# VectorE's transposition behind the hidden low parts, and another pacing wait ahead of the loop's down projection, in a one-core block kernel

## The chip, the cores and the metric

The kernel runs on one core of a Trainium2 chip. Its engines each take their own list of instructions in order and meet only at semaphores: TensorE (PE; its weight loads are listed as PEld), VectorE (DVE), ScalarE (ACT), GpSimd (POOL), and SyncE (SP), which issues most of the DMAs. The metric is the device time of one execution in microseconds (us). The kernel before took 506.76 us, the median of three runs from 506.46 to 507.39.

## The reference: what is computed

The input x has 8 sequences of 1024 tokens of 256 features, all float32. Two residual blocks follow each other:

```
x = x + mixer(layernorm(x))
x = x + experts(layernorm(x))

mixer:   xp, z = split(x @ w_in)                  # 256 -> 2 x 512
         xc = silu(depthwise causal convolution of xp, 4 taps, + conv_b)
         h[t] = 0.9 * h[t-1] + 0.1 * (xc[t] @ w_B) # 16 states, a scan over the tokens
         y = (h @ w_C) * silu(z)
         return y @ w_out                          # 512 -> 256
experts: per sequence, the two best of 8 experts by (first token @ Wr + br)
         mean over both of  gelu(x @ W1 + b1) @ W2 + b2
```

## The kernel before, in words

**Precision.** A float32 product is made of three products of a rounded type: each operand is split into a high part (rounded, on ACT) and a low part (the rest, by a subtraction), and PE adds hi x hi, hi x lo and lo x hi. So nearly every tensor that PE reads has a `_hi`, made by ACT, and a `_lo`, made by DVE or POOL. The state's input and output (`state_in`, `state_out`) pack high and low parts into one operand, `b_mix`, `c_mix` and `state_mix`.

**Chunks and steps.** The 8192 tokens are 16 chunks (NC) of 512 tokens, two per sequence. The work is a software pipeline over steps s: in step s, chunk a = s is in the mixer, chunk o = s - 1 has its output projection, residual and second layernorm, and chunk f = s - 2 is in the experts. An opening handles the first chunks; steps 4 to 13 are a hardware loop of five rounds (each an even step, q = 0, then an odd one, q = 1); step 3 and steps 14 to 17 are written out. In the profile step s = 3 reaches down at 100.7 us, step 4 at 131.4, step 8 at 252.9, step 9 at 283.1 and step 14 at 434.9.

**PE's order in a step** (`step` at the end of `tensor`): `xp` (input projection, x half), `out_proj` of chunk o in two halves, `z` (the gate half), `up` of chunk f, `state_in` (four products of `b_mix` with `xc_hi`, L1486, and four with `xc_lo`, L1489), `down` of chunk f: its first half (24 products of 256 columns), 12 products of its second half, then `state_out` (four products, L1510), then down's last 12 products. `down(f, 0, ...)`'s products are L1422 to L1424, in groups of three; 36 of them stand ahead of `state_out` and 12 behind. `down` waits for `g_lo` (the low parts of the hidden layer, `hid_lo`), `state_out` for `h_lo` (the low part of `state_mix`).

**The pacing waits.** PE's instructions are issued ahead of their execution. In front of the first product of `out_proj` and of `down`, PE waits for one of its own earlier products (`behind` with a constant in the written-out steps, `behind_next` with a register in the loop) and then issues a few increments of a semaphore, `paced`, that nobody waits for. `state_tail` is incremented by the first of the four L1489 products, the fourth-last of `state_in`. A wait directly ahead of an increment becomes one instruction with it. So in the loop two semaphore instructions and one register instruction stand between that product's end and down's first weight load, in the written-out steps three semaphore instructions.

**DVE's order in a step** (`step` in `vector`), from the residual on: `residual`, `turn2_lo`, `stats2`, then `stats1` and `moments1` of chunk a + 2, `turn_squares(a + 1)` (L971: transposes the 32 x 32 squares of the normalized chunk that a DMA has regrouped; ACT's `turn1_hi` reads it), `hidden_lo(f)` (four subtractions, L861, each behind ACT's `hid_hi` of that part), `scan(a)` (L1041, the recurrence), `edge` (a small copy), `state_lo(a)` (L861 again, the low part of `state_mix`), `turn1_lo(a + 1)`, `ys(a)` and `finish(f)`. L861 is the line of a helper: the tiles' names tell its uses apart.

**ACT's order** behind the gates: a table load, then for each of four parts the gelu (L728) and its rounding `hid_hi` (L611), `norm2(o)` (L666, four), `state_hi(a)` (L611, `state_mix`, behind the scan), `turn1_hi(a + 1)`. **POOL** in even steps adds `b_sel` to the residual (L498, four) behind all four `hid_lo`; in odd steps it does so earlier, between its other work.

**The chain inside a step** is thus: gelu and `hid_hi` on ACT, `hid_lo` and scan on DVE, `state_hi` on ACT, `state_lo` on DVE, `state_out` on PE.

Of the kernel before, what the change touches and what calls it, by code (L numbers as in the profile page):

```python
# [22 lines left out]
def build_block(nc, x, w_in, conv_w, conv_b, w_B, w_C, w_out, Wr, br, W1, b1, W2, b2, out):  # L23
# [19 lines left out]
    with ExitStack() as ctx:  # L43
# [129 lines left out]


        passed = sem("passed")
        x_tail, state_tail, up_tail = sem("x_tail"), sem("state_tail"), sem("up_tail")
        paced = sem("paced")

# [680 lines left out]
        def _(dve):  # L859
# [286 lines left out]
            def step(s, q, half):  # L1146
                a, o, f = s, s - 1, s - 2
                halves = half - 1 if q == 0 else half
                if q == 0 and not has_attn(s):
                    last_split((1, 2, 3))  # L1150
                    route(half - 1)
                    finish(f - 1, 1, 1)
                    turn2_lo(f)
                    residual(o, 1, halves, 0)
                    residual(o, 1, halves, 1)
                    stats2(o, 1)
                    hidden_lo(f, range(JF))
                    norm2_last()
                    turn2_lo(o)
                    finish(f, 0, 0)  # L1160
                    finish(f, 0, 1)
                    return
                if q == 0:
                    route(half - 1)
                    if has_attn(s):
                        taps(a, 0)
                    turn_squares2(f)
                    if has_attn(s):
                        taps(a, 1)
                    residual(o, 1, halves, 0)  # L1170
                    residual(o, 1, halves, 1)
                    turn2_lo(f)
                    stats2(o, 1)
                    if has_next(s, 2):
                        stats1(a + 2)
                        moments1(a + 2)
                    if has_next(s, 1):
                        turn_squares(a + 1)
                    hidden_lo(f, range(JF))
                    if has_attn(s):  # L1180
                        scan(a, 0)
                    if has_next(s, 1):
                        edge(a + 1, False)
                    if has_attn(s):
                        state_lo(a, 0)
                    if has_next(s, 1):
                        turn1_lo(a + 1)
                    if has_attn(s):
                        ys(a)
                    finish(f, 0, 0)  # L1190
                    finish(f, 0, 1)
                    return
                if not has_attn(s):
                    hidden_lo(f, range(JF))
                    finish(f, 1, 0)
                    finish_tile(f, 1, 2, tok[1])
                    finish_tile(f, 1, 3, turn[0])
                    return
                taps(a, 0)
                if isinstance(a, int) and a == 3:  # L1200
                    taps(a, 1)
                    turn_squares2(f)
                    turn2_lo(f)
                else:
                    turn_squares2(f)
                    taps(a, 1)
                residual(o, 0, halves, 0)
                residual(o, 0, halves, 1)
                if not (isinstance(a, int) and a == 3):
                    turn2_lo(f)  # L1210
                stats2(o, 0)
                if has_next(s, 2):
                    stats1(a + 2)
                if has_next(s, 2):
                    moments1(a + 2)
                if has_next(s, 1):
                    turn_squares(a + 1)
                hidden_lo(f, range(JF))
                scan(a, 1)
                if has_next(s, 1):  # L1220
                    edge(a + 1, True)
                state_lo(a, 1)
                if has_next(s, 1):
                    turn1_lo(a + 1)
                if has_next(s, 1):
                    ys(a)
                    finish(f, 1, 0)
                    finish(f, 1, 1)
                else:
                    finish(f, 1, 0)  # L1230
                    ys(a)
# [5 lines left out]
        def _(pe):  # L1237
            mm = nc.tensor.matmul
            x_nth, state_nth = nc.tensor.alloc_register("x_nth"), nc.tensor.alloc_register("state_nth")
            nc.tensor.reg_mov(x_nth, FIRST + 1)  # L1240
            nc.tensor.reg_mov(state_nth, FIRST + 1)

            def turns(normed, sem_out):
                for k in range(KD):
# [188 lines left out]
            def behind_next(tail, nth):  # L1433
# [3 lines left out]
                    pe.sem_inc(paced, 1)  # L1437
                nc.tensor.reg_add(nth, nth, 1)

            def down_tile(f, n, dst, js=range(JF)):  # L1440
                rows = slice(n * P, (n + 1) * P)
                for j in js:
                    t, cols = j // KD, slice(j % KD * D, (j % KD + 1) * D)
                    mm(dst, hid_hi[:, j, rows], w2_hi[:, t, cols], start=(j == 0), stop=False)
                    mm(dst, hid_hi[:, j, rows], w2_lo[:, t, cols], start=False, stop=False)
                    ins = mm(dst, hid_lo[:, j, rows], w2_hi[:, t, cols], start=False, stop=(j == JF - 1))
                if js[-1] == JF - 1:
                    ins.then_inc(down_ready, 1)

            def down(f, h, js=range(JF), tail=None):  # L1450
                for j in js:
                    if h == 0:
                        pe.wait_ge(g_lo, f * JF + j + 1)
                        if isinstance(f, int) and f == LAST - 1 and j % KD == 0:
                            pe.wait_ge(w2_lo_set, LAST // 2 * TOP_K + j // KD + 1)
                    if j == 0 and tail is not None:
                        if isinstance(f, int):
                            behind(*tail)
                        else:
                            behind_next(state_tail, state_nth)  # L1460
                    t, cols = j // KD, slice(j % KD * D, (j % KD + 1) * D)
                    ins = tokens(h, j, j == JF - 1, hid_hi, hid_lo, w2_hi[:, t, cols], w2_lo[:, t, cols])
                if js[-1] == JF - 1:
                    ins.then_inc(down_ready, 1)
# [17 lines left out]
            def state_in(a):  # L1482
                bank = u_bank(a)
                for j in range(JD):
                    pe.wait_ge(xc_hi_set, a * JD + j + 1)
                    mm(bank[:], b_mix[:, j, :], xc_hi[:, j, :], start=(j == 0), stop=False)  # L1486
                for j in range(JD):
                    pe.wait_ge(xc_lo_set, a * JD + JD if isinstance(a, int) and a < 3 else a * JD + j + 1)
                    ins = mm(bank[:], b_mix[:, j, :], xc_lo[:, j, :], start=False, stop=(j == JD - 1))  # L1489
                    if j == JD - 4:  # L1490
                        ins.then_inc(state_tail, 1)
                ins.then_inc(u_ready, 1)
# [167 lines left out]
```

## Time and profile before

| | |
|---|---|
| median of three runs | 506.76 us (506.46 to 507.39) |
| the profiled execution | 505.8 us, its span 504.0 us |
| granted clock of PE | 0.999 |
| busy: PE, DVE, ACT, POOL | 99%, 90%, 79%, 69% |
| the products' L1510 (`state_out`) | 395 ns mean |
| L1422 in `down` and in `out_proj` | 281 and 278 ns mean |

The span runs from the first to the last instruction of the profiled execution; its own time is 1.8 us longer. Busy time of an engine counts its execution only, with overlapping products counted once. A product's listed duration contains its filling and draining, so products start more closely than they last: the start-to-start distances in the timelines are what PE's time is made of. The same holds for DVE, where an instruction starts a little before the end of the one ahead of it.

### The profile page before, as it was taken

What the parts mean: (1) busy time and instruction counts of PE and PEld (TensorE: products, weight loads), DVE (VectorE), ACT (ScalarE), POOL (GpSimd) and SP (SyncE); (2) the same over time, 40 slices, a digit from 0 to 9 for tenths busy, and PEclk for the clock granted to TensorE, in tenths of its full rate; (3) what the DMA queues carried; (4) which work ended last, traced back from release to release, by engine and by line L of the source; (5) the groups of instructions that cost most, each with busy time, mean ns of one, the idle gap of its engine ahead of it and who ended that gap; (6) DMA issues with size and microseconds to landing.
All of it is one profiled execution on the core that took longest, in us unless ns stands there. A gap on an engine that the chain in (4) does not pass through costs nothing.

```text
span 504.0 us, 9945 instructions
## 1 busy us (share of the span) xinstructions
PE 498.7 (99%) x3026; PEld 440.4 (87%) x3026; DVE 452.9 (90%) x896; ACT 400.2 (79%) x692; POOL 348.7 (69%) x390
## 2 busy tenths in 40 slices
PE   8999999999999999999999999999999999999997
PEld 7888799788888988888888888988889888888997
DVE  6999999989998899989999899998999989996773
ACT  4986959878869788697887969779797888969554
POOL 4959597559693696928969197782977649764291
PEclk9999999999999999999999999999999999999999
DMA  8940105344151532605235160432604333130102
GB/s 259 298 179 6 37 1 179 114 142 153 64 190 42 167 125 83 208 10 199 82 125 166 42 221 28 165 126 83 208 31 136 125 126 126 47 120 1 42 2 85
DMA packets 53380, 57.29 MB, mean 114 GB/s; under 512 B 8682, under 2 KB 49642, under 8 KB 53226
## 3 DMA queue, kind: packets, MB, share of 16 engines
q1 hardware_dynamic: 51498, 56.67, 33.7%
q10 hardware_dynamic: 1856, 0.31, 0.3%
q8 instruction: 13, 0.21, 0.2%
q14 instruction: 13, 0.11, 0.1%
HBM read 35.46 MB, written 21.50 MB: 113 GB/s over the span
## 4 chain that ended last, share of the span: by engine, by line
PE 98%; DVE 1%; DMA 1%; issue 0%; DVEq 0%
PE blk L1299 16%; PE blk L1302 16%; PE blk L1308 16%; PE tok L1422 12%; PE tok L1424 12%; PE tok L1423 11%; PE blk L1510 3%; PE turn L1489 3%; PE turn L1486 3%; PE turn L1246 1%; PE tok L1308 1%; PE tok L1302 1%; PE tok L1299 1%; DMA x_mid<-in_L_attn_x 1%; DVE stats_t L917 0%; DVE normed L934 0%
## 5 line engine op out<-in xcount | busy, mean ns | idle before, releaser
L992 DVE SCALAR_TENSOR_TENSOR conv<-blk,tap_w,conv 128x512 f32<-128x512 f32 x192 | 130.1, 742 | 7.2 <-ACT conv L683 6.3
L488 POOL TENSOR_TENSOR y_lo<-gate,y_hi 128x512 fp32r<-128x512 f32 x57 | 72.2, 1297 | 35.9 <-ACT y_hi L611 35.8
L1299 PE MATMUL blk<-xn_hi,w_in_hi 128*128 128x512 f32 x228 | 89.6, 393 | 0.0
L1302 PE MATMUL blk<-xn_hi,w_in_lo 128*128 128x512 f32 x228 | 89.0, 390 | 0.0
L453 POOL TENSOR_TENSOR xc_lo<-conv,xc_hi 128x512 fp32r<-128x512 f32 x60 | 73.2, 1236 | 7.5 <-ACT xc_hi L611 7.4
L1422 PE MATMUL tok<-w_out_hi,y_hi 128*128 128x256 f32 x256 | 71.1, 278 | 0.0
L1423 PE MATMUL tok<-w_out_lo,y_hi 128*128 128x256 f32 x256 | 70.8, 276 | 0.0
L1424 PE MATMUL tok<-w_out_hi,y_lo 128*128 128x256 f32 x256 | 70.7, 276 | 0.0
L1308 PE MATMUL blk<-xn_lo,w_in_hi 128*128 128x512 f32 x228 | 70.4, 390 | 0.0
L1422 PE MATMUL tok<-w_hi,hid_hi 128*128 128x256 f32 x248 | 69.8, 281 | 0.2
L1424 PE MATMUL tok<-w_hi,hid_lo 128*128 128x256 f32 x248 | 69.3, 279 | 0.0
L1423 PE MATMUL tok<-w_lo,hid_hi 128*128 128x256 f32 x248 | 69.3, 279 | 0.0
L683 ACT ACTIVATE conv<-blk,tap_b,tap_w 128x512 f32<-128x512 f32 x64 | 49.1, 777 | 24.8 <-PE blk L1308 21.4
L689 ACT ACTIVATE conv<-conv 128x512 f32<-128x512 f32 x64 | 39.3, 630 | 30.5 <-DVE conv L992 29.5
L861 DVE TENSOR_TENSOR hid_lo<-hid,hid_hi 128x512 fp32r<-128x512 f32 x64 | 44.8, 732 | 15.5 <-ACT hid_hi L611 15.2
L498 POOL TENSOR_TENSOR x_mid<-x_mid,b_sel 128x256 f32<-128x256 f32 x60 | 45.7, 794 | 13.2 <-DVE hid_lo L861 11.2
L1308 PEld LDWEIGHTS blk<-xn_lo,w_in_hi 128*128 128x128 f32 x228 | 42.8, 188 | 9.1
L1422 PEld LDWEIGHTS tok<-w_out_hi,y_hi 128*128 128x128 f32 x256 | 48.0, 188 | 2.6 <-issue 1.3
L1302 PEld LDWEIGHTS blk<-xn_hi,w_in_lo 128*128 128x128 f32 x228 | 42.8, 188 | 8.0
L1299 PEld LDWEIGHTS blk<-xn_hi,w_in_hi 128*128 128x128 f32 x228 | 42.8, 188 | 8.1
L1422 PEld LDWEIGHTS tok<-w_hi,hid_hi 128*128 128x128 f32 x248 | 46.6, 188 | 3.7 <-issue 2.2
L1299 PE MATMUL blk<-xn_hi,w_hi 128*128 128x512 f32 x124 | 48.4, 390 | 0.0
(189 smaller groups left out, 1320.5 us busy)
## 6 DMA issues: line engine op xcount, KB each, us to landing
spill<-normed SPq DMA_DIRECT2D x25, 512.0 KB, 2.9
normed<-spill SPq DMA_DIRECT2D x100, 128.0 KB, 2.8
out<-x_mid SPq DMA_DIRECT2D x30, 256.0 KB, 2.4
x_mid<-in_L_attn_x SPq DMA_DIRECT2D x29, 256.0 KB, 2.8
x_in<-in_L_attn_x SPq DMA_DIRECT2D x14, 512.0 KB, 3.8
w_all<-in_L_ffn_W SPq DMA_DIRECT2D x2, 2048.0 KB, 11.3
b_all<-in_L_ffn_b SPq DMA_DIRECT2D x1, 1024.0 KB, 13.9
gate<-in_L_attn_w_in SPq DMA_DIRECT2D x2, 256.0 KB, 4.8
```

The lines of the kernel that those rows point to most:

```text
L453: nc.gpsimd.tensor_tensor(xc_lo[:, j, :], conv[:, j, 0:CH], xc_hi[:, j, :].bitcast(F32), ALU.subtract).then_inc(xc_lo_set, 1)
L488: nc.gpsimd.tensor_tensor(y_lo[:, j, :], gate_of(o, j), y_hi[:, j, :].bitcast(F32), ALU.subtract).then_inc(y_lo_set, 1)
L498: ins = nc.gpsimd.tensor_tensor(mid(f, q)[:, n, :], mid(f, q)[:, n, :], b2_sel[:], ALU.add)
L683: nc.scalar.activation(conv[:, j, HALO:HALO + CH], blk[j][:], ACT.Identity, bias=tap_b[:, j:j + 1], scale=tap_w[:, j, 0:1]).then_inc(tap_f ...
L861: return nc.vector.tensor_tensor(dst, src, hi.bitcast(F32), ALU.subtract)
L992: nc.vector.scalar_tensor_tensor(cols, blk[j][:], tap_w[:, j, t:t + 1], cols, ALU.mult, ALU.add).then_inc(tap_added, 1)
L1299: ins = mm(dst, whi(k), his(k), start=(k == 0), stop=False)
L1302: mm(dst, wlo(k), his(k), start=False, stop=False)
L1308: ins = mm(dst, whi(k), los(k), start=False, stop=(k == KD - 1))
L1422: mm(dst, his[:, j, rows], whi, start=(j == 0 and n == 0), stop=False, skip_group_check=True)
L1423: mm(dst, his[:, j, rows], wlo, start=False, stop=False, skip_group_check=True)
L1424: ins = mm(dst, los[:, j, rows], whi, start=False, stop=(last and n == 1), skip_group_check=True)
```

## The change

Two edits. On DVE, in both kinds of step, `hidden_lo(f, range(JF))` is issued ahead of `turn_squares(a + 1)` instead of behind it (the diff shows the even one). On PE, in the loop alone, `down` waits for another product: the fourth of the four L1486 products increments the new semaphore `state_fifth` by 2; `behind_fifth` counts a register up by one, waits for `state_fifth`, issues three increments, counts the register up again, and waits once more (for the same increment by 2) with one more increment. The written-out steps keep `behind` and `state_tail`.

```
-                    if has_next(s, 1):
-                        turn_squares(a + 1)
                     hidden_lo(f, range(JF))
+                    if has_next(s, 1):
+                        turn_squares(a + 1)
                     if has_attn(s):
                         scan(a, 0)
...
-            nc.tensor.reg_mov(state_nth, FIRST + 1)
+            nc.tensor.reg_mov(state_nth, 0)
...
+            def behind_fifth(tail, nth):
+                pe.sem_inc(paced, 1)
+                nc.tensor.reg_add(nth, nth, 1)
+                pe.wait_ge(tail, nth)
+                for _ in range(PACE):
+                    pe.sem_inc(paced, 1)
+                nc.tensor.reg_add(nth, nth, 1)
+                pe.wait_ge(tail, nth)
+                pe.sem_inc(paced, 1)
...
-                            behind_next(state_tail, state_nth)
+                            behind_fifth(state_fifth, state_nth)
...
-                    mm(bank[:], b_mix[:, j, :], xc_hi[:, j, :], start=(j == 0), stop=False)
+                    ins = mm(bank[:], b_mix[:, j, :], xc_hi[:, j, :], start=(j == 0), stop=False)
+                if not isinstance(a, int):
+                    ins.then_inc(state_fifth, 2)
```

## Rows read from the trace of the kernel before

**Rows 1.** Page, parts 1 and 4: busy time of TensorE; chain of work by engine.

```profile
PE 498.7 (99%) x3026; PEld 440.4 (87%) x3026; DVE 452.9 (90%) x896; ACT 400.2 (79%) x692; POOL 348.7 (69%) x390
...
PE 98%; DVE 1%; DMA 1%; issue 0%; DVEq 0%
```

**Rows 2.** Timeline of VectorE, step 9: start, us taken, operation, count, [idle before].

```profile
278.95 1.24 DVE L971 STREAM_TRANSPOSE normed<-normed 128x1024 f32<-128x1024 f32 x1
280.11 1.27 DVE L861 TENSOR_TENSOR hid_lo<-hid,hid_hi 128x512 fp32r<-128x512 f32 x2
...
283.17 0.69 DVE L861 TENSOR_TENSOR hid_lo<-hid,hid_hi 128x512 fp32r<-128x512 f32 x1 [0.55 <-ACT hid_hi L611]
283.78 1.27 DVE L1041 TENSOR_TENSOR_SCAN state<-decay,state,turn 128x512 f32<-128x512 f32 x1
...
285.75 0.69 DVE L861 TENSOR_TENSOR state_mix<-state,state_mix 64x512 fp32r<-64x512 f32 x1 [0.63 <-ACT state_mix L611]
```

**Rows 3.** Timeline of ScalarE, step 9: the fourth hid_hi, and state_mix.

```profile
282.51 0.63 ACT L611 ACTIVATE hid_hi<-hid 128x512 fp32r<-128x512 f32 x1
...
285.09 0.63 ACT L611 ACTIVATE state_mix<-state 128x512 fp32r<-128x512 f32 x1
```

**Rows 4.** Timeline of TensorE, step 9: down, state_out, down's last 12.

```profile
283.13 0.28 PE L1422 MATMUL tok<-w_hi,hid_hi 128*128 128x256 f32 x1
...
287.37 1.09 PE L1510 MATMUL blk<-state_mix,c_mix 128*128 128x512 f32 x4
288.29 0.28 PE L1422 MATMUL tok<-w_hi,hid_hi 128*128 128x256 f32 x1
```

**Rows 5.** Timeline of VectorE, step 8.

```profile
251.52 2.47 DVE L861 TENSOR_TENSOR hid_lo<-hid,hid_hi 128x512 fp32r<-128x512 f32 x4
253.92 1.21 DVE L1041 TENSOR_TENSOR_SCAN state<-decay,turn 128x512 f32<-128x512 f32 x1
...
255.83 1.03 DVE L861 TENSOR_TENSOR state_mix<-state,state_mix 64x512 fp32r<-64x512 f32 x1 [0.18 <-ACT state_mix L611]
```

**Rows 6.** Timeline of ScalarE, step 8: the fourth hid_hi.

```profile
252.29 0.63 ACT L611 ACTIVATE hid_hi<-hid 128x512 fp32r<-128x512 f32 x1
```

**Rows 7.** Timeline of TensorE, step 8: state_out and down's last 12.

```profile
257.15 1.09 PE L1510 MATMUL blk<-state_mix,c_mix 128*128 128x512 f32 x4
258.08 0.28 PE L1422 MATMUL tok<-w_hi,hid_hi 128*128 128x256 f32 x1
```

**Rows 8.** Timelines of VectorE and TensorE, step 6.

```profile
195.18 1.02 DVE L861 TENSOR_TENSOR state_mix<-state,state_mix 64x512 fp32r<-64x512 f32 x1 [0.20 <-ACT state_mix L611]
...
197.27 0.28 PE L1422 MATMUL tok<-w_hi,hid_hi 128*128 128x256 f32 x1
```

**Rows 9.** Line L971 alone: count, shortest/median/longest in ns, first and last start.

```profile
L971 DVE STREAM_TRANSPOSE normed<-normed x12: 1231/1235/1240, 98.3 to 429.6; 128x1024 f32<-128x1024 f32 x12
```

**Rows 10.** Timelines of TensorE and ScalarE, step 14.

```profile
434.94 0.28 PE L1422 MATMUL tok<-w_hi,hid_hi 128*128 128x256 f32 x1
...
439.06 1.09 PE L1510 MATMUL blk<-state_mix,c_mix 128*128 128x512 f32 x4
...
434.32 0.63 ACT L611 ACTIVATE hid_hi<-hid 128x512 fp32r<-128x512 f32 x1
```

**Rows 11.** Timelines of ScalarE and TensorE, step 4.

```profile
130.49 0.63 ACT L611 ACTIVATE hid_hi<-hid 128x512 fp32r<-128x512 f32 x1
...
131.40 0.35 PE L1422 MATMUL tok<-w_hi,hid_hi 128*128 128x256 f32 x1
...
136.65 0.28 PE L1422 MATMUL tok<-w_hi,hid_hi 128*128 128x256 f32 x1
```

**Rows 12.** Timeline of GpSimd, step 8: its four adds.

```profile
254.16 3.29 POOL L498 TENSOR_TENSOR x_mid<-x_mid,b_sel 128x256 f32<-128x256 f32 x4 [2.05 <-DVE hid_lo L861]
```

**Rows 13.** Timeline of VectorE, start of step 8: a tap waits for ScalarE.

```profile
233.00 0.75 DVE L992 SCALAR_TENSOR_TENSOR conv<-blk,tap_w,conv 128x512 f32<-128x512 f32 x1 [0.61 <-ACT conv L683]
```

**Rows 14.** Line L1437 alone, a semaphore instruction of the pacing: ns, starts.

```profile
L1437 PEldq EVENT_SEMAPHORE  x40: 51/51/51, 112.4 to 404.1; - x40
```

More of the change, by code:

```diff
@@ L175, in build_block @@
         passed = sem("passed")
+        state_fifth = sem("state_fifth")
         x_tail, state_tail, up_tail = sem("x_tail"), sem("state_tail"), sem("up_tail")
@@ L1176, in step @@
                         moments1(a + 2)
+                    hidden_lo(f, range(JF))
                     if has_next(s, 1):
                         turn_squares(a + 1)
-                    hidden_lo(f, range(JF))
                     if has_attn(s):
@@ L1215, in step @@
                     moments1(a + 2)
+                hidden_lo(f, range(JF))
                 if has_next(s, 1):
                     turn_squares(a + 1)
-                hidden_lo(f, range(JF))
                 scan(a, 1)
```

## The prediction

> **What bounds the kernel now.** Read the chain of work that ended last first: TensorE (PE) holds 98% of it [rows 1], so what counts is only what leaves PE idle or slows its products. VectorE (DVE) is no bound of its own, but every hand-over inside a step goes through it. Steps are named by s = a, as in the code (s = 4 to 13 are the loop). All sums below are made inside one step, from the timelines, on the stretch from the end of ScalarE's (ACT) fourth hid_hi to the start of down's last 12 products (first L1422 after L1510).
>
> Odd step s = 9, in order of time. DVE does the transposition L971, then hid_lo (four L861), idles 0.55 us before the last of them until ACT's fourth hid_hi is there, then scan L1041, then the low part of state_mix [rows 2]. ACT ends the fourth hid_hi at 283.14 and rounds state_mix from 285.09 [rows 3]. PE starts down at 283.13, state_out at 287.37 and down's last 12 at 288.29 [rows 4]. The low part of state_mix is ready at 285.75 + 0.69 = 286.44, 0.93 us before state_out takes it. That 0.93 is the cover that matters. In the even step s = 8 it is 257.15 - 256.86 = 0.29 (state_out starts 0.93 before 258.08) [rows 5, 7].
>
> How close may it get? In s = 6 the low part ends at 195.18 + 1.02 = 196.20 and down's last 12 start at 197.27 [rows 8]: 1.07 after it. In s = 9 that distance is 288.29 - 286.44 = 1.85. State_out's four products alone take 0.92 (288.29 - 287.37), so in s = 6 PE went on 0.15 after the data, and I take 1.07 as the price from the data to PE going on.
>
> **Part 1, hidden_lo ahead of turn_squares.** Nothing is added; DVE's order changes from L971, L861 x4, L1041 to L861 x4, L971, L1041, in every step from 3 to 14 (12 transpositions, 1.235 us each [rows 9]). In the odd step the transposition now runs in time in which DVE would otherwise wait for ACT: it ends before hid_lo, and the fourth hid_lo starts 0.03 after ACT's fourth hid_hi. That instant is ACT's and does not move. Behind it the new order puts the whole transposition, 280.11 - 278.95 = 1.16 us start to start, in front of the scan.
>
> The new sum for an odd step, from the end of the fourth hid_hi: 0.03 to hid_lo's start (283.14 to 283.17), 0.61 to the next DVE instruction (283.17 to 283.78), 1.16 for the transposition, 1.27 for the scan, 0.04 to ACT (285.05 to 285.09), 0.63 for its rounding, 0.03 back to DVE, 0.69 for the low part, 1.07 for state_out [rows 2, 3, 8]. Together 5.53 us. Before it was 288.29 - 283.14 = 5.15. So 0.38 us is lost on PE in each odd step: the 1.16 less the unused cover.
>
> Even step: the scan takes 1.21 instead of 1.27 [rows 5], so the new stretch is 5.47. Before: s = 8 258.08 - 252.92 = 5.16 [rows 6, 7], loss 0.31; s = 6, 10 and 12 were not worked out one by one; s = 14, by its rows, 439.06 + 0.92 - 434.95 = 5.03, loss 0.44 [rows 10]. I take the middle, 0.37, for each of the five (6, 8, 10, 12, 14). s = 4 is another case: down starts only at 131.40, late against ACT's fourth hid_hi at 131.12, since hid_lo is late there; the old stretch is 136.65 - 131.12 = 5.53 [rows 11]. The new order takes that lateness away and puts the other in its place: -0.06. s = 3 has no row here; with a late hid_lo too, its bounds are -0.06 (as s = 4) and 0.38 (as an odd step); I take 0.2.
>
> One thing decides what an even step costs. Its low part of state_mix takes 1.03 us instead of the odd step's 0.69, with GpSimd's (POOL) four adds L498 running from 254.16 to 257.45 beside it [rows 5, 12]; in the odd step POOL does them elsewhere. The adds start 0.17 after the last hid_lo (253.99). In the new order the last hid_lo ends at 252.95 + 0.69 = 253.64, so the adds run from 253.81, 0.35 earlier, and end at 257.1 at the latest, while the low part starts later, at 256.63 instead of 255.83. I take 0.69; with the old duration it is 0.34 more per even step. Bounds: 0.69 and 1.03. The Trainium skill, SBUF — State Buffer, "Who interferes with whom", says of this case that a VectorE instruction with two SBUF inputs and a GpSimd one that reads SBUF exclude each other, and the one issued second waits for the whole of the first. The trace agrees with a wait of that kind (0.34 us more); by this rule the low part would run free once the adds are through, and be held about as long as the fourth add still has to run, which puts the even step between my two bounds.
>
> Who else waits for DVE? The transposed normed1 is read by ACT's turn1_hi, which stands behind state_hi in ACT's order, and state_hi itself waits for the scan: no further wait. After state_out DVE's xn_lo, ys and finish come later by about what PE comes later, and in front of its next taps DVE waits 0.61 us for ACT [rows 13], which takes up the rest. SP and POOL lose no time in front of PE: no DMA is issued at another place in its queue. Cost: 0; without that cover, see the rivals.
>
> **Part 2, the pacing wait of down in the loop.** Ten times, PE waits for the fourth high product, which is one product (0.23 us, 0.92 for four) earlier than before, and then has four semaphore instructions (the waiting one counted) and one register instruction where it had two and one, and one register instruction more ahead of the wait. Each semaphore instruction is 51 ns in its row [rows 14]; what it holds the queue for is not seen. Bounds for the start of down: earlier than now by 0.23 - 0.10 = 0.13, with which down runs as now; or later by 0.2. The aim can be read from PE's rows: the 36 products before state_out take 287.37 - 283.13 = 4.24 in the loop, but 439.06 - 434.94 = 4.12 in s = 14, which has three semaphore instructions and no register instruction [rows 4, 10]. So a gain up to 0.12 per step, 1.1 in nine steps. But it lies ahead of state_out, and state_out now waits for the low part: in the odd step ready at 283.14 + 5.53 - 1.07 = 287.60, where down ends at 287.37 + 0.2 at the latest. Gain and loss both disappear in the wait. I take 0.
>
> **Sum.** Odd 5 x 0.38 = 1.9, even 5 x 0.37 = 1.85, s = 3 +0.2, s = 4 -0.06: 3.9 us. The profiled execution took 505.8 us with a span of 504.0; the span would become 507.9. The median of the runs shown is 506.76, 0.96 above the profiled one; the difference is added to it: 510.7.
>
> **The rivals.**
> 1. *Contention stays.* The low part of state_mix takes 1.03 in all six even steps: 6 x 0.34 = 2.0 more, 512.7. For it: all even steps shown have it. Against: the adds move forward, the low part back.
> 2. *The transposition is hidden after all (the other side).* The place is state_out's wait for the low part of state_mix. It decides at the point where that is ready 0.1 to 0.3 us ahead of state_out's planned start. If the delay stayed below the cover (0.93), PE would keep its beat, the late starts of s = 3 and 4 would go (5.53 - 5.15 = 0.38, and 0.2), and the pacing could bring its 1.1: 505.1, faster; without the pacing 506.2, the same. For it: DVE idles 0.55 before its last hid_lo. Against: that idle time is before the fourth hid_lo, and 1.16 is more than 0.93.
> 3. *The delay accumulates.* DVE carries it into its taps and PE waits in the next step as well; nothing of it is covered. At the full 1.16 for six odd steps (3 with them) and 253.92 to 254.72, 0.80, for six even ones: 11.8 us, 518.6. Against: the 0.61 us in front of the taps, and PE itself is later.
> 4. *The change does not pace.* The new wait passes too early: as said, no time.
>
> **How the numbers follow.** Forecast with rival 4: 0.73. Rival 1: 0.12. Rival 3: 0.05. Rival 2: 0.10, of which 0.06 with the pacing (faster) and 0.04 without (same). Less than 0.2% (1.0 us) cannot be told from no change here. Faster 0.06, same 0.04, slower 0.90. Low end: 1.07 could be 0.1 less with PE's queue empty, 11 x 0.1 = 1.1 less, and s = 3 at nothing: 509.4. High end: rival 1 and a little: 512.9.
>
> **What would show it.** DVE's timeline: L971 between the fourth hid_lo and L1041, the scan of odd steps 1.80 instead of 0.64 us after the fourth hid_hi. PE's waits: a new entry, L1510 (or its weight load) for DVE's state_mix, some 0.4 us each in about 11 steps; the share of PE busy falls below 99%. POOL's adds in even steps end before or at the start of the low part, which is 0.69. If L1510 shows no wait, or if PE's lost time sits at L1299 or L1422 of the next step, the forecast is wrong.

## The result, and the profile after

The changed kernel took 513.63 us, the median of four runs (512.02 to 514.2), against 506.77 (506.46 to 507.39, four runs) of the kernel before: a ratio of 1.0129, 95% interval 1.0104 to 1.0153. It is slower by 6 to 7 us; forecast were 3.9, with 512.9 us as the high end. The profiled execution took 512.02 us, its span is 510.2 instead of 504.0: 6.2 more, and this is what the sums below account for. The other three executions took 513.59 to 514.2; they were not traced, and the 0.6 us between 6.2 and the 6.9 of the medians stays open. The granted clock was 0.999 before and 1.000 after, so it is not the clock. Lines behind the edits are numbered higher after: L971 is L972, L861 is L862, L1041 is L1042, L1422 to L1424 are L1423 to L1425, L1510 is L1524.

The page after: the span, busy times, and the chain of work by engine. Those of before are [rows 1].

```profile
span 510.2 us, 9985 instructions
...
PE 501.6 (98%) x3026; PEld 439.7 (86%) x3026; DVE 451.7 (89%) x896; ACT 399.9 (78%) x692; POOL 346.7 (68%) x390
...
PE 59%; DVE 20%; issue 10%; ACT 9%; DMA 1%; DVEq 0%
```

TensorE held 98% of the chain; now it holds 59%, because in every step the chain leaves TensorE for VectorE's `hid_lo`, transposition and scan, ScalarE's rounding and VectorE's low part. In step 9 it comes to them from ScalarE's gelu; in step 8 it is on ScalarE and VectorE almost throughout from 234.3 us, where the taps wait for the input projection. The waits say where it comes back. Of TensorE and its weight loads the first two rows for `state_out` are these (us in all, times, the longest); before there was none for this line.

```profile
PE blk L1524 <- DVE state_mix L862: 3.0, 10, 0.4
...
PEld blk L1524 <- DVE state_mix L862: 5.5, 12, 0.6
```

**An odd step**, s = 9, VectorE's timeline (start, us taken, operation, count, [idle before]). It answers to [rows 2].

```profile
284.88 0.69 DVE L862 TENSOR_TENSOR hid_lo<-hid,hid_hi 128x512 fp32r<-128x512 f32 x1 [0.55 <-ACT hid_hi L612]
286.12 0.69 DVE L862 TENSOR_TENSOR hid_lo<-hid,hid_hi 128x512 fp32r<-128x512 f32 x1 [0.55 <-ACT hid_hi L612]
286.73 1.24 DVE L972 STREAM_TRANSPOSE normed<-normed 128x1024 f32<-128x1024 f32 x1
287.90 1.24 DVE L1042 TENSOR_TENSOR_SCAN state<-decay,state,turn 128x512 f32<-128x512 f32 x1
...
289.83 0.69 DVE L862 TENSOR_TENSOR state_mix<-state,state_mix 64x512 fp32r<-64x512 f32 x1 [0.63 <-ACT state_mix L612]
```

And TensorE's, which answers to [rows 4]:

```profile
290.58 1.21 PE L1524 MATMUL blk<-state_mix,c_mix 128*128 128x512 f32 x4 [0.22 <-DVE state_mix L862]
291.63 0.28 PE L1423 MATMUL tok<-w_hi,hid_hi 128*128 128x256 f32 x1
```

The fourth `hid_hi` ends at 286.09, so down's last 12 start 5.54 behind it, by the rounded rows. All five odd steps of the loop give 5.52 to 5.53. The forecast was 5.53.

**An even step**, s = 8, VectorE's timeline, which answers to [rows 5]. `state_in`'s first product starts at 253.16 here and at 251.09 before.

```profile
252.25 0.86 DVE L886 TENSOR_SCALAR neg_mean<-mean_var 128x4 f32<-128x4 f32 x1
253.03 0.16 DVE L887 TENSOR_SCALAR var_eps<-mean_var 128x4 f32<-128x4 f32 x1
253.10 3.24 DVE L862 TENSOR_TENSOR hid_lo<-hid,hid_hi 128x512 fp32r<-128x512 f32 x4
256.26 1.23 DVE L972 STREAM_TRANSPOSE normed<-normed 128x1024 f32<-128x1024 f32 x1
257.42 1.17 DVE L1042 TENSOR_TENSOR_SCAN state<-decay,turn 128x512 f32<-128x512 f32 x1
...
259.30 0.69 DVE L862 TENSOR_TENSOR state_mix<-state,state_mix 64x512 fp32r<-64x512 f32 x1 [0.64 <-ACT state_mix L612]
```

TensorE's, which answers to [rows 7], and ScalarE's fourth `hid_hi`, which answers to [rows 6]:

```profile
260.04 1.20 PE L1524 MATMUL blk<-state_mix,c_mix 128*128 128x512 f32 x4 [0.30 <-DVE state_mix L862]
261.07 0.28 PE L1423 MATMUL tok<-w_hi,hid_hi 128*128 128x256 f32 x1
```

```profile
254.36 0.63 ACT L612 ACTIVATE hid_hi<-hid 128x512 fp32r<-128x512 f32 x1
```

The stretch is 261.07 - 254.99 = 6.08 us, where 5.47 was forecast and 5.16 was before. The transposition starts 1.27 us behind the end of the fourth `hid_hi` (256.26 against 254.99), not 0.64 as in the odd step. Everything behind it takes what the forecast gave it within 0.05 us, the low part of `state_mix` with its 0.69 included. So the excess is ahead of the transposition: four `hid_lo` take 3.24 us without a pause where they took 2.47, and they start late.

GpSimd in the same stretch shows who is beside them:

```profile
231.31 5.08 POOL L489 TENSOR_TENSOR y_lo<-gate,y_hi 128x512 fp32r<-128x512 f32 x4 [1.89 <-ACT y_hi L612]
...
251.80 1.29 POOL L454 TENSOR_TENSOR xc_lo<-conv,xc_hi 128x512 fp32r<-128x512 f32 x1
253.04 0.74 POOL L481 TENSOR_TENSOR b_sum<-b_all 128x256 f32 x1
253.98 1.06 POOL L484 TENSOR_SCALAR b_sel<-b_sum 128x256 f32<-128x256 f32 x1 [0.20 <-POOL b_sum L481]
```

In this and all sums below a time "relative to `state_in`" is that time less the start of the step's first `state_in` product. The same places before, GpSimd first, then VectorE:

```profile
228.52 5.06 POOL L488 TENSOR_TENSOR y_lo<-gate,y_hi 128x512 fp32r<-128x512 f32 x4 [1.05 <-ACT y_hi L611]
...
249.06 1.29 POOL L453 TENSOR_TENSOR xc_lo<-conv,xc_hi 128x512 fp32r<-128x512 f32 x1
250.31 0.74 POOL L480 TENSOR_TENSOR b_sum<-b_all 128x256 f32 x1
```

```profile
249.52 0.86 DVE L885 TENSOR_SCALAR neg_mean<-mean_var 128x4 f32<-128x4 f32 x1
...
250.36 1.23 DVE L971 STREAM_TRANSPOSE normed<-normed 128x1024 f32<-128x1024 f32 x1
```

Two things are to be seen. First, the last `xc_lo` starts at -2.03 before and at -1.36 after: GpSimd is 0.67 us later against TensorE. Its `y_lo`, at the step's start, is already 0.71 later (228.52 - 251.09 = -22.57, 231.31 - 253.16 = -21.85), and waits for ScalarE's `y_hi`, which hangs on the previous, odd step's late scan. Second, VectorE's small `neg_mean`, which takes 0.17 us alone, takes 0.86 until GpSimd's `xc_lo` ends, before and after; so VectorE gets to the next instruction at -0.73 before (250.36) and at -0.06 after (253.10). The same happens once more ahead of it: the second layernorm's `var_eps` (L913) takes 1.07 us after, until the `xc_lo` before that ends, and 0.16 before, where its `neg_mean` is held to 0.35; behind it VectorE is at -3.53 before and at -2.86 after. Twice VectorE is set back to GpSimd's time. The instruction at -0.73 was the transposition, 1.23 us long beside `b_sum`. Now it is `hid_lo`, and the first takes 1.24 us and the second 0.88, where 0.65 to 0.69 is their length in the loop before. The trace of before already had such a case in s = 14, where the transposition is through early and the `hid_lo` meet `xc_lo`, `b_sum` and `b_sel`: they take 1.68, 1.22, 0.88 and 0.69.

```profile
431.27 4.42 DVE L861 TENSOR_TENSOR hid_lo<-hid,hid_hi 128x512 fp32r<-128x512 f32 x4 [0.42 <-ACT hid_hi L611]
```

Step by step, the stretch before and after: s = 3 5.34 and 5.52; s = 4 5.53 and 6.02; s = 6, 8, 10, 12 together 20.47 and 24.18; the five odd steps together 25.78 and 27.64; s = 14 5.02 and 5.55. That is 6.75 more. From `state_in` of s = 3 to that of s = 15 the time grows by 6.18 (364.65 to 370.83); 0.57 comes back between the stretches. Of this, 0.50 lies in down's last 12 products: 1.36 to 1.38 us from the first of them to the next product after, but for s = 14, and 1.41 in every step before.

### The profile page after: what moved, and what is told of

It reads as the page before. It is cut to its first block, busy times and chain, and to the rows that moved or that the text cites. A ratio compares the mean times of both kernels' runs of the same rounds, so it can differ in the third digit from the quotient of the medians.

```text
span 510.2 us, 9985 instructions
## 1 busy us (share of the span) xinstructions
PE 501.6 (98%) x3026; PEld 439.7 (86%) x3026; DVE 451.7 (89%) x896; ACT 399.9 (78%) x692; POOL 346.7 (68%) x390
## 4 chain that ended last, share of the span: by engine, by line
PE 59%; DVE 20%; issue 10%; ACT 9%; DMA 1%; DVEq 0%
PE blk L1300 9%; PE blk L1303 9%; PE blk L1309 9%; PE tok L1423 7%; PE tok L1424 7%; PE tok L1425 7%; PE blk L1524 3%; ACT hid L729 3%; DVE hid_lo L862 3%; DVE conv L993 3%; DVE normed L972 3%; DVE state L1042 2%; DVE xn_lo L862 2%; ACT hid_hi L612 2%; DVE state_mix L862 2%
## 5 line engine op out<-in xcount | busy, mean ns | idle before, releaser
L454 POOL TENSOR_TENSOR xc_lo<-conv,xc_hi 128x512 fp32r<-128x512 f32 x60 | 71.8, 1214 | 8.9 <-ACT xc_hi L612 8.8
L1423 PE MATMUL tok<-w_out_hi,y_hi 128*128 128x256 f32 x256 | 71.1, 278 | 0.0
L1425 PE MATMUL tok<-w_out_hi,y_lo 128*128 128x256 f32 x256 | 70.7, 276 | 0.0
L1424 PE MATMUL tok<-w_out_lo,y_hi 128*128 128x256 f32 x256 | 70.7, 276 | 0.0
L1423 PE MATMUL tok<-w_hi,hid_hi 128*128 128x256 f32 x248 | 69.8, 281 | 0.4
L862 DVE TENSOR_TENSOR hid_lo<-hid,hid_hi 128x512 fp32r<-128x512 f32 x64 | 49.1, 790 | 23.0 <-ACT hid_hi L612 22.8
L1424 PE MATMUL tok<-w_lo,hid_hi 128*128 128x256 f32 x248 | 68.9, 278 | 0.0
L1425 PE MATMUL tok<-w_hi,hid_lo 128*128 128x256 f32 x248 | 68.8, 278 | 0.0
L1423 PEld LDWEIGHTS tok<-w_hi,hid_hi 128*128 128x128 f32 x248 | 46.6, 188 | 4.8 <-issue 4.2
L1423 PEld LDWEIGHTS tok<-w_out_hi,y_hi 128*128 128x128 f32 x256 | 48.0, 188 | 2.6 <-issue 1.3
L499 POOL TENSOR_TENSOR x_mid<-x_mid,b_sel 128x256 f32<-128x256 f32 x60 | 43.0, 749 | 9.5 <-DVE hid_lo L862 4.5
```

The costliest lines, as they stand in the source:

```text
L454: nc.gpsimd.tensor_tensor(xc_lo[:, j, :], conv[:, j, 0:CH], xc_hi[:, j, :].bitcast(F32), ALU.subtract).then_inc(xc_lo_set, 1)
L499: ins = nc.gpsimd.tensor_tensor(mid(f, q)[:, n, :], mid(f, q)[:, n, :], b2_sel[:], ALU.add)
L862: return nc.vector.tensor_tensor(dst, src, hi.bitcast(F32), ALU.subtract)
L1423: mm(dst, his[:, j, rows], whi, start=(j == 0 and n == 0), stop=False, skip_group_check=True)
L1424: mm(dst, his[:, j, rows], wlo, start=False, stop=False, skip_group_check=True)
L1425: ins = mm(dst, los[:, j, rows], whi, start=False, stop=(last and n == 1), skip_group_check=True)
```

## The experiments

Each is compared with the kernel before on the same chip. The kernel before had a median of 506.06 us in the launch of the first four, 506.61 in that of the next four, 506.45 and 506.73 in the last two.

**1. Only the order, old pacing.** `hidden_lo` ahead of `turn_squares` in both kinds of step; `behind_next` stays.

```
+                    hidden_lo(f, range(JF))
                     if has_next(s, 1):
                         turn_squares(a + 1)
-                    hidden_lo(f, range(JF))
```

> The new order of VectorE, the old pacing wait. My theory: state_out waits for the low part of state_mix in every step, so the pacing ahead of it moves nothing; the time is that of the changed kernel, 513.3 (512.5 to 514.0). Rival (part of the loss is the later start of down in even steps, caused by the longer pacing sequence behind a late g_lo): 1.0 to 1.5 us less than the changed kernel, about 512.

Measured: 512.62 us, ratio 1.0125 (1.0108 to 1.0142). Odd stretches 5.51 to 5.52, even 6.04 to 6.07. With the new order the pacing carries none of the loss and hides none.

**2. Only the pacing.** `behind_fifth` and `state_fifth` as in the change, the old order.

> The old order of VectorE, the new pacing wait. In odd steps the first load of down starts some 0.14 us after the last product of state_in instead of 0.11, the 36 products take 4.12 instead of 4.24: -0.6 us in five steps. In even steps hid_lo comes late and the longer sequence (0.86 us from the wait for g_lo to the load in the changed kernel) starts down 0.2 to 0.35 later: +0.9 to +1.5 in five steps. Together 507.4 (506.8 to 507.9). Rival (the pacing is a gain everywhere): 505.6.

Measured: 507.09 us, 1.0019 (1.0009 to 1.0028). TensorE's timelines around down's start, even step s = 8, first the products, then the weight loads:

```profile
252.51 1.07 PE L1503 MATMUL turn<-xc_lo,b_mix 128*128 128x512 f32 x4
253.71 0.36 PE L1423 MATMUL tok<-w_hi,hid_hi 128*128 128x256 f32 x1
```

```profile
253.68 0.19 PEld L1423 LDWEIGHTS tok<-w_hi,hid_hi 128*128 128x128 f32 x1 [0.52 <-issue]
```

Down's first product starts 1.20 us behind `state_in`'s fifth instead of 0.91 (252.00 to 252.91 before): 0.27 to 0.29 late in the even steps 6 to 12 (s = 4 was as late before), and the 36 products behind it take 4.18 or 4.32. In odd steps the start is in time, and the 36 products take 4.13 instead of 4.24 in four of the five. The loss of the even steps and the gain of the odd ones partly cancel, as long as no late `state_out` waits behind them; in the changed kernel it does, and both go into its wait.

**3 and 4. The order in one kind of step only**, both with the new pacing: odd_only leaves the even step's order as before, even_only the odd step's.

> The new order in odd steps (3 to 13) alone, the new pacing. Theory (a late odd step is carried into the even one: GpSimd and VectorE reach its hid_lo 0.67 us later, measured against PE): odd steps lose 0.34 each as in the changed kernel, and even steps, although their order is the old one, lose another 0.2 to 0.5 each: 509.6 (509.0 to 510.6). Rival (each step's loss comes from its own order alone): 1.7 + 0.2 for the odd ones and the even ones' pacing loss of about 1: at most 509.0, and no shift of the even steps' scan against PE.

Measured: 512.03 us, 1.0117 (1.01 to 1.0134). Odd stretches are again 5.52. But the even ones, whose own order is that of before, take 5.92 to 6.04. Their VectorE rows, s = 8 (`state_in` at 253.72), TensorE's first product of down and of its last 12, and the waits of TensorE for `hid_lo` in all:

```profile
253.66 1.23 DVE L972 STREAM_TRANSPOSE normed<-normed 128x1024 f32<-128x1024 f32 x1
254.82 2.48 DVE L862 TENSOR_TENSOR hid_lo<-hid,hid_hi 128x512 fp32r<-128x512 f32 x4
257.23 1.21 DVE L1042 TENSOR_TENSOR_SCAN state<-decay,turn 128x512 f32<-128x512 f32 x1
...
259.13 1.02 DVE L862 TENSOR_TENSOR state_mix<-state,state_mix 64x512 fp32r<-64x512 f32 x1 [0.20 <-ACT state_mix L612]
```

```profile
256.46 0.36 PE L1423 MATMUL tok<-w_hi,hid_hi 128*128 128x256 f32 x1 [0.77 <-DVE hid_lo L862]
...
261.57 0.28 PE L1423 MATMUL tok<-w_hi,hid_hi 128*128 128x256 f32 x1
```

```profile
PE tok L1423 <- DVE hid_lo L862: 3.7, 5, 0.8
```

VectorE is at -0.06 again: the odd steps' lateness comes over although nothing in the even step was edited. In the old order the transposition still stands in front of `hid_lo`, so the first `hid_lo` starts at 1.11 instead of 0.43, and it is down's first product that waits: it starts 2.75 us behind `state_in`'s first, 1.82 before. Of these 0.93 us about 0.67 is the lateness; the rest is the size of the 0.29 that the longer pacing costs behind a late `hid_lo` in run 2. `state_out` then waits for nothing, and the loss is of another kind than in the changed kernel, where down starts 2.10 behind and `state_out` waits. The measured 6.0 us over the kernel before in this launch was more than I expected: the carrying over was in that expectation, its size was too small.

> The new order in even steps (4 to 14) alone, the new pacing. Theory (hid_lo now shares the SBUF port with GpSimd's b_sum and b_sel; the transposition did not): even steps lose 0.5 to 0.6 each even without lateness carried from the odd step: the first hid_lo takes over 1.0 us instead of 0.69; odd steps gain 0.12 by the pacing: 508.9 (508.2 to 509.8). Rival (the surplus of the even steps is only carried over from the odd ones): even steps lose my forecast 0.31 to 0.37 each, 507.7, and the first hid_lo takes 0.69.

Measured: 507.75 us, 1.0035 (1.0022 to 1.0047). VectorE, s = 8 (`state_in` at 251.59), and down's last 12:

```profile
250.92 3.24 DVE L862 TENSOR_TENSOR hid_lo<-hid,hid_hi 128x512 fp32r<-128x512 f32 x4
254.08 1.23 DVE L972 STREAM_TRANSPOSE normed<-normed 128x1024 f32<-128x1024 f32 x1
```

```profile
258.89 0.28 PE L1423 MATMUL tok<-w_hi,hid_hi 128*128 128x256 f32 x1
```

The first `hid_lo` is held to 1.23 and the second to 0.88 just as in the changed kernel, and the four take the same 3.24. But VectorE arrives at -0.67, so the transposition starts at 2.49, and the stretch is 5.47 to 5.50 in s = 6 to 12: the forecast's 5.47. My expectation charged the holding with more; alone it costs at most 0.03 there. The rival's number, 507.7, came out, but not its reason, an unheld `hid_lo`. s = 4 is the exception, 5.95: there VectorE arrives at -0.23 although step 3 was not reordered, as it came late in the kernel before (-0.30). So in s = 6 to 12 the holding alone does not explain the changed kernel's 6.08: it must meet the lateness. The next two runs take one half each out of the changed kernel.

**5. The holding taken away.** The changed kernel, with GpSimd's `b_sum` and `b_sel` on 8 of 256 columns in the loop's even steps; the bias of the chosen experts is stale in the other columns.

```
+                n = D if isinstance(seq, int) else 8
-                nc.gpsimd.tensor_tensor(b2_sum[:], rows[0], rows[1], ALU.add).then_inc(b2_set, 1)
+                nc.gpsimd.tensor_tensor(b2_sum[:, 0:n], rows[0][:, 0:n], rows[1][:, 0:n], ALU.add).then_inc(b2_set, 1)
...
-                nc.gpsimd.tensor_scalar(b2_sel[:], b2_sum[:], 1.0 / TOP_K, None, ALU.mult).then_inc(b2_set, 1)
+                nc.gpsimd.tensor_scalar(b2_sel[:, 0:n], b2_sum[:, 0:n], 1.0 / TOP_K, None, ALU.mult).then_inc(b2_set, 1)
```

> The changed kernel; in the loop's even steps GpSimd's b_sum and b_sel work on 8 of 256 columns (the chosen bias of the other columns is stale). Theory (the surplus of the even steps needs two causes at once: VectorE reaches hid_lo 0.67 us late, carried from the odd step, and the first two hid_lo are held 0.55 and 0.20 us by b_sum and b_sel): without the holding the fourth hid_lo starts with ACT again, 1.86 us after state_in's first product instead of 2.40 to 2.50, the stretch from ACT's fourth hid_hi to down's last 12 falls from 6.0-6.1 to 5.5 in five steps: 2.7 us less than the changed kernel, a ratio of 1.007 to 1.008. Rival (the lateness alone does it): the stretch stays at or above 5.9, ratio 1.012.

Measured: 510.85 us, 1.0085 (1.007 to 1.0101). VectorE, s = 8 (`state_in` at 252.71), and down's last 12:

```profile
252.58 2.69 DVE L863 TENSOR_TENSOR hid_lo<-hid,hid_hi 128x512 fp32r<-128x512 f32 x4
255.19 1.24 DVE L973 STREAM_TRANSPOSE normed<-normed 128x1024 f32<-128x1024 f32 x1
```

```profile
260.00 0.28 PE L1424 MATMUL tok<-w_hi,hid_hi 128*128 128x256 f32 x1
```

VectorE still arrives late, at -0.13, but no `hid_lo` is held (2.69 with the wait for ScalarE in it), the transposition starts at 2.48, and the stretch is 5.46 to 5.47, s = 4 included.

**6. The lateness taken away.** The changed kernel, with GpSimd's `w2_lo` on 64 of 512 columns in the loop's even steps (the low parts of the second weights are stale in the rest), so that GpSimd comes earlier to `xc_lo` and `b_sum`.

```
+                    n = KD * D if isinstance(seq, int) else D // 4
-                    nc.gpsimd.tensor_tensor(w2_lo[:, t, :], raw, w2_hi[:, t, :].bitcast(F32),
+                    nc.gpsimd.tensor_tensor(w2_lo[:, t, 0:n], raw[:, 0:n], w2_hi[:, t, 0:n].bitcast(F32),
```

> The changed kernel; in the loop's even steps GpSimd's two subtractions for w2_lo work on 64 of 512 columns (the rest is stale), 2 us less of GpSimd's unbroken chain from y_lo to b_sel. b_sum and b_sel stay whole. Theory (VectorE is late because GpSimd is late: y_lo starts 0.7 later after the odd step, and VectorE's small instructions wait for GpSimd's subtraction xc_lo): VectorE reaches hid_lo 0.7 us earlier or more in even steps, the fourth hid_lo starts at 1.86 to 1.95, the stretch falls to 5.5: a ratio of 1.007 to 1.008. Rival (VectorE is late by its own work, from state_lo to the taps): it stays late, -0.07 instead of -0.73 against state_in's first product, ratio 1.012.

Measured: 510.9 us, 1.0092 (1.0077 to 1.0108). VectorE, s = 8 (`state_in` at 253.11), and down's last 12:

```profile
251.25 1.93 DVE L863 TENSOR_TENSOR hid_lo<-hid,hid_hi 128x512 fp32r<-128x512 f32 x2
253.73 0.69 DVE L863 TENSOR_TENSOR hid_lo<-hid,hid_hi 128x512 fp32r<-128x512 f32 x1 [0.55 <-ACT hid_hi L613]
254.97 0.69 DVE L863 TENSOR_TENSOR hid_lo<-hid,hid_hi 128x512 fp32r<-128x512 f32 x1 [0.55 <-ACT hid_hi L613]
```

```profile
260.41 0.28 PE L1424 MATMUL tok<-w_hi,hid_hi 128*128 128x256 f32 x1
```

The first `hid_lo` still takes 1.1, but it starts 1.86 us ahead of `state_in`, and the fourth waits for ScalarE as in an odd step. This edit takes more away than the lateness: GpSimd is 1.9 us earlier, and only the first `hid_lo` is still held, by 0.4. Stretches 5.46 to 5.47. Either half taken out gives back all of the excess in the stretches, 2.9 us over all steps. The ratios fall by less, from 1.0129 to 1.0085 and 1.0092, which is 2.2 and 1.9 us where 2.7 was expected; the intervals reach about 1 us to either side. That both times, 510.85 and 510.9, lie close to the 510.7 forecast for the whole change follows from the stretches, which are now those of the forecast, and not from a forecast of these kernels.

**7. Control for 5.** The kernel before with the same small `b_sum` and `b_sel`, the bias stale in the same columns.

> Control: the kernel before, with b_sum and b_sel on 8 of 256 columns in the loop's even steps (stale beyond). Behind the transposition hid_lo meets them no more, so less work on GpSimd gives nothing: ratio 0.999 to 1.001. Rival (less GpSimd work is worth time by itself): 0.997 or less.

Measured: 506.31 us, 0.9995 (0.9986 to 1.0005). The lighter adds are worth nothing by themselves in the old order.

**8 to 10. Can the pacing alone bring what its faster mode of down promises?** All keep the old order. pace_ahead moves wait, three increments and a register instruction ahead of down's wait for `g_lo`; pace_ahead2 has one increment more; reg_first has the old wait for `state_tail`, but counts the register ahead of it and leaves only semaphore instructions behind it.

```
+            def behind_ahead(tail, nth):
+                nc.tensor.reg_add(nth, nth, 1)
+                pe.wait_ge(tail, nth)
+                for _ in range(PACE):
+                    pe.sem_inc(paced, 1)
+                nc.tensor.reg_add(nth, nth, 0)
```

```
+            def behind_first(tail, nth):
+                pe.sem_inc(paced, 1)
+                nc.tensor.reg_add(nth, nth, 1)
+                pe.wait_ge(tail, nth)
+                for _ in range(PACE):
+                    pe.sem_inc(paced, 1)
```

> Tried for a kernel better than both: the old order of VectorE, and in the loop the pacing (wait for the fifth-last product, three semaphore instructions, one register instruction) put ahead of the wait for g_lo, which so becomes the last semaphore instruction in front of down's first load. Theory: the load starts 0.14 to 0.15 us after state_in's last product in odd and even steps, the 36 products take 4.12 instead of 4.24 in seven steps, the late starts of steps 4 and 6 go: -1.0 us, ratio 0.998 (0.997 to 0.999). Rival (which start is good depends on the phase in which a launch runs, and the old wait is good in half of them): 0.999 to 1.000.

> As pace_ahead, where the wait for g_lo turned out to ride on the first weight load and not to be an instruction of its own, so that down's first load came 0.05 to 0.09 us after state_in's last product and its products kept the 0.118 spacing: one more increment of the semaphore in its place. Theory (a first load some 0.14 to 0.16 us after the last product gives the 0.113 spacing in every launch): load at +0.144 in odd, +0.144 to +0.165 in even steps, 36 products in 4.12, ratio 0.997 to 0.999. Rival (no gain beyond what the old pacing gives in about half of the launches): 0.999 to 1.000.

> The kernel before, with the loop's pacing in the form of the written-out steps: the register is counted up ahead of the wait, and three semaphore instructions follow. The first load of down starts 0.128 after state_in's last product in odd steps, 0.13 to 0.2 in even ones. Written-out steps with this delay showed 4.11 for the 36 products in some launches and 4.25 in others, by the phase in which the launch ran. Theory: the same here, no reliable gain, ratio 0.998 to 1.000, and the profile shows all odd steps in one of the two modes. Rival (the loop's two-and-one form is itself the slower one): 0.998 with 4.11 in all odd steps.

Measured: 507.06 us, 1.0006 (0.9997 to 1.0015); 506.74, 1.0008 (0.9999 to 1.0017); 507.2, 1.0016 (1.0007 to 1.0025). None is faster; the gain expected of the first two did not come, and reg_first lies above both of its ranges. In the loop down's first load comes 0.05 to 0.09 us behind the start of `state_in`'s last product in pace_ahead, 0.06 (odd) and 0.20 (even, but for s = 4) in pace_ahead2, and 0.13 in four of reg_first's odd steps, and the 36 products take 4.24 or 4.25 us in nearly all of these steps all the same. The exceptions are pace_ahead's s = 5 with 4.08, pace_ahead2's even steps with 4.16 in s = 8, 10 and 12, 4.20 in s = 4 and 4.32 in s = 6, and reg_first's s = 5, where the load comes at 0.16 and they take 4.13.

**11 and 12. The transposition moved only as far as its cover reaches.** behind_scan puts it behind the scan instead of in front of it, in both kinds of step, with the old pacing; behind_scan_even in even steps only.

```
-                    if has_next(s, 1):
-                        turn_squares(a + 1)
                     hidden_lo(f, range(JF))
                     if has_attn(s):
                         scan(a, 0)
...
+                    if has_next(s, 1):
+                        turn_squares(a + 1)
```

> The kernel before, with the transposition one place further on than in the changed kernel: hidden_lo, scan, turn_squares, then edge and state_lo; old pacing. It now lies beside ACT's rounding of state_mix. Theory (what costs is the transposition between ACT's fourth hid_hi and the scan, 1.16 us on the state's chain; behind the scan 0.63 of it are hidden): the low part of state_mix starts some 0.4 to 0.5 us later in odd steps, within the cover of 0.93; in even steps the scan comes up to 0.3 earlier and the low part is about as early as before; ys and so GpSimd's y_lo are 0.4 late into the even step. Ratio 0.999 to 1.001. Rival (any transposition behind hidden_lo costs, since the lateness carried into the even step decides): 1.004 or more.

Measured: 509.49 us, 1.0061 (1.0047 to 1.0075), where no change was expected. The odd steps lose nothing, as expected; they take 4.98 to 5.02, less than the 5.16 of before, since down's 36 products take 4.08 or 4.11 in them here and 4.24 there. The even ones take 5.82 to 5.88; VectorE, s = 8 (`state_in` at 251.87):

```profile
251.68 3.24 DVE L861 TENSOR_TENSOR hid_lo<-hid,hid_hi 128x512 fp32r<-128x512 f32 x4
254.85 1.21 DVE L1041 TENSOR_TENSOR_SCAN state<-decay,turn 128x512 f32<-128x512 f32 x1
255.98 1.21 DVE L971 STREAM_TRANSPOSE normed<-normed 128x1024 f32<-128x1024 f32 x1
257.29 1.19 DVE L861 TENSOR_TENSOR state_mix<-state,state_mix 64x512 fp32r<-64x512 f32 x1
```

VectorE comes 0.5 us late (-0.19 instead of -0.73), brought over from the odd step as in odd_only (with the even steps edited alone, next run, it is at -0.67), presumably by its transposition in front of `ys`; the first two `hid_lo` are held as before; and the low part of `state_mix` takes 1.19 beside GpSimd's adds. These are the same mechanisms, lateness brought over and a held instruction, now met in front of the scan and once more behind it.

> The same in even steps alone; odd steps keep the transposition ahead of hidden_lo, where VectorE would idle. Theory: nothing is carried late into the even step, down starts on time in steps 4 and 6 (0.3 us and less), the low part of state_mix starts where it did: ratio 0.998 to 1.000. Rival (hid_lo held by b_sum and b_sel takes the gain back in the low part's start): 1.000 to 1.002.

Measured: 507.55 us, 1.0019 (1.001 to 1.0028), which is the rival's range. Even stretches are 5.38 (s = 4: 5.79), with a low part of 1.18. No kernel tried beats the one before.

## Why the prediction was wrong

**What held.** The odd step's sum, 5.53 forecast and 5.52 to 5.53 measured, with every term at its place: transposition 1.17 start to start, scan 1.24 where 1.27 was taken, low part 0.69. The price of 1.07 from the low part's end to the last 12 is 1.11 here (290.52 to 291.63), so two misses of 0.03 and 0.04 cancel. The low part of even steps takes 0.69, so rival 1 did not happen. In the changed kernel it also starts later than forecast; even_only, where it starts where the forecast had it, shows 0.69 too. Nor did rival 2: the 0.55 us of idle time [rows 2] still stands ahead of the fourth `hid_lo` (286.12), where the transposition behind it cannot use it. Part 2 is worth nothing beside part 1, as order_only against the changed kernel shows (1.0125 and 1.0129, each against the kernel before). The wait at `state_out` appeared in 12 steps.

**What failed.** The step "Who else waits for DVE? ... SP and POOL lose no time in front of PE ... Cost: 0", and with it "the fourth hid_lo starts 0.03 after ACT's fourth hid_hi" as taken for even steps. GpSimd does lose time: the late scan makes `ys` and ScalarE's `y_hi` late, GpSimd's `y_lo` waits for it, and in an even step GpSimd has no pause from there to `b_sum` in which to take it up. It hands 0.67 us on to VectorE through `var_eps` and `neg_mean`; the holding of `neg_mean` stands in the trace of before as well. The 0.61 us in front of the taps [rows 13], which I took for cover, lies on VectorE, not on GpSimd.

The second half of the step is that the reordering exchanges neighbours. Beside `b_sum` and `b_sel` stood the transposition, which takes 1.23 there as everywhere [rows 9]; now two `hid_lo` stand there and take 0.55 and 0.20 more. The prediction looked for such an exchange at one place, the low part of `state_mix`, and not at the place where the moved instruction had been; the `hid_lo` of s = 14, held up to 1.68 us in the trace of before, were a sign of it. The rule of the Trainium skill (SBUF — State Buffer, "Who interferes with whom"), that two such instructions exclude each other, was thus applied to the low part alone. These rows agree with it: the first `hid_lo` starts 0.06 us behind `b_sum` (253.10, 253.04) and takes 0.55 more.

The two cost time only beyond the cover. In s = 8 they are 0.67 + 0.55 + 0.20 = 1.42 us; about 0.8 of it would be idle time ahead of the fourth `hid_lo`, and 0.63 remains (1.27 - 0.64). With one of the two alone nothing or nearly nothing remains in s = 6 to 12, as runs 5 and 6 show and even_only confirms. In s = 4 the holding needs no lateness from a reordered step, since VectorE is late there in the kernel before. So:

| stretches | forecast | measured |
|---|---|---|
| five odd steps | +1.9 | +1.86 |
| s = 6, 8, 10, 12 | +1.48 | +3.71 |
| s = 4 | -0.06 | +0.49 |
| s = 14 | +0.37 | +0.53 |
| s = 3 | +0.2 | +0.18 |

The excess of the five even steps of the loop is 2.23 + 0.55 = 2.8 us, and it is the term that was mis-sized: the forecast put their loss at 1.4 us together, and 4.2 was measured. s = 14 is 0.16 over the value taken and 0.09 over its own estimate of 0.44; its transposition starts 0.09 later than an odd step's, behind a fourth `hid_lo` of 0.77. Rival 3 named the kind of mechanism, a delay handed on to the next step, but put it at 11.8 us and on VectorE's taps; measured, it decides at the even step's fourth `hid_lo`. The odd steps take up what the even ones hand on: their stretches don't exceed the forecast.

**Open.** Why down's last 12 products run faster behind a `state_out` that has waited, and why the untraced executions of the changed kernel took 1.6 to 2.2 us more than the traced one.

## What to carry to other kernels

When an instruction is moved, look at who takes its old place as well as at its new one: here the new neighbour is held up by another engine's adds and the old one was not. Follow each delayed result through all engines to the next step, and count an idle time as cover only if it lies on the way that the delay takes. Two delays that are each within the cover can exceed it together, so test them one at a time by taking either away.

## What the runs showed of the hardware

Down's 36 products have two paces behind the same instructions: 4.24 us in most steps of the loop before [rows 4], 4.08 to 4.13 in other steps and kernels, or 0.1178 against 0.1133 us per product at 4.24 and 4.08. Where the first load comes 0.17 us or more behind `state_in`'s last product, the first products start further apart, and the 36 take 4.15 to 4.32. Here is before_small_b2, s = 9, weight load and product; the next rows are those of reg_first, also s = 9.

```profile
282.90 0.19 PEld L1423 LDWEIGHTS tok<-w_hi,hid_hi 128*128 128x128 f32 x1
...
283.01 0.28 PE L1423 MATMUL tok<-w_hi,hid_hi 128*128 128x256 f32 x1
```

```profile
283.13 0.19 PEld L1422 LDWEIGHTS tok<-w_hi,hid_hi 128*128 128x128 f32 x1 [0.16 <-issue]
...
283.23 0.28 PE L1422 MATMUL tok<-w_hi,hid_hi 128*128 128x256 f32 x1
```

The load comes 0.11 and 0.10 us ahead of its product; the first ran all 36 products in 4.08 us, the second in 4.25. In steps 3 to 15 of all fourteen traces, told by the median distance from product to product, a load 0.10 to 0.13 us behind the start of `state_in`'s last product was followed by the faster pace 41 times and by the slower 33 times, and by both within one trace (order_only: slower in s = 8, faster in s = 10, the load at 0.11 in both). With 0.14 to 0.16 it was the faster all 44 times, with 0.17 the slower 15 times in 16. Single executions of the kernel before lie between 505.2 and 507.4 us. Whether the two paces make this spread was not shown, since one execution of each kernel was traced; a pacing edit worth 1 us is half as large as the spread.
